# Attention of a four-layer kernel: tiles 8 to 15 are added to the four partial sums by accumulating DMAs, and the totals and the output product change slots

## What is computed

```python
scores = jnp.einsum('bhsd,bhtd->bhst', q, k) * scale
attn = jax.nn.softmax(scores, axis=-1)
o = jnp.einsum('bhst,bhtd->bhsd', attn, v_c)
o = o.transpose(0, 2, 1, 3).reshape(b, s, N_HEADS * D_K)
return o @ W_O + b_O
```

## Time and profile before

| | us |
|---|---|
| three runs | 737.27, 737.66, 738.73 |
| median | 737.66 |
| span of the profiled execution | 737.8 |
| attention loop in it, first score to last | 38.1 to 484.4 |

### The profile page before, as it was taken

How to read it: one execution, slowest core, us unless ns; L and a number is a source line. 1 busy time by engine, 2 the same in 40 slices (tenths; PEclk the granted TensorE clock), 3 DMA queues, 4 the chain that set the end, 5 groups by cost and what they waited for, 6 DMA issues and landing times.

```text
span 737.8 us, 12518 instructions
## 1 busy us (share of the span) xinstructions
PE 718.6 (97%) x4180; PEld 469.0 (64%) x4180; DVE 629.4 (85%) x1304; ACT 466.1 (63%) x1069; POOL 583.5 (79%) x484
## 2 busy tenths in 40 slices
PE   8999999999999999999999999999899999999997
PEld 7665655655656656556556555466666699778885
DVE  8889999999999999999999899765978736878885
ACT  4367766766767767767667676654777831455553
POOL 6489989999999999999989999963689861446774
PEclk9999999999999999999999999999999999999999
DMA  6300000000000000000000000012000000032431
GB/s 148 91 1 2 1 2 2 2 3 2 1 2 2 1 2 3 1 1 2 2 1 3 2 1 2 2 46 74 2 1 0 2 1 1 1 87 74 141 103 28
DMA packets 40679, 15.57 MB, mean 21 GB/s; under 512 B 27292, under 2 KB 36525, under 8 KB 40616
## 3 DMA queue, kind: packets, MB, share of 16 engines
q1 hardware_dynamic: 39336, 14.67, 8.2%
q10 hardware_dynamic: 1280, 0.12, 0.1%
HBM read 13.35 MB, written 1.10 MB: 20 GB/s over the span
## 4 chain that ended last, share of the span: by engine, by line
PE 74%; POOL 11%; issue 7%; DVE 6%; ACT 1%; DMA 0%; POOLq 0%; DVEq 0%
PE ps L1482 17%; PE ps L1468 16%; PE ps L1526 15%; POOL hid_lo L1007 5%; PE ps L1510 4%; PE ps L1880 4%; PE ps L1537 3%; POOL nrm L987 2%; DVE mx L1061 2%; PE ps L1920 2%; PE ps L1922 1%; PE ps L1921 1%; POOL hid L987 1%; PE ps L1455 1%; PE ps L1456 1%
## 5 line engine op out<-in xcount | busy, mean ns | idle before, releaser
L1061 DVE TENSOR_REDUCE mx<-ps 128x1 f32<-128x512 f32 x492 | 302.6, 681 | 14.7 <-PE ps L1468 13.2
L622 ACT ACTIVATE prob<-ps 128x512 f32<-128x512 f32 x512 | 262.7, 630 | 9.2 <-PE ps L1482 9.1
L1482 PE MATMUL ps<-q_cols,key 128*128 128x512 f32 x512 | 209.5, 412 | 0.8 <-ACT prob L622 0.8
L1468 PE MATMUL ps<-key,q_rows 128*128 128x512 f32 x512 | 204.7, 404 | 0.8 <-DVE key L1047 0.4
L901 POOL TENSOR_TENSOR part<-part,prob 128x512 f32<-128x512 f32 x124 | 158.6, 1290 | 30.4 <-DVE part L1076 25.9
L1482 PEld LDWEIGHTS ps<-q_cols,key 128*128 128x128 f32 x512 | 95.4, 187 | 89.5 <-issue 50.7
L1526 PE MATMUL ps<-prob,val 128*32 128x512 f32 x1024 | 124.1, 598 | 0.0
L1468 PEld LDWEIGHTS ps<-key,q_rows 128*128 128x128 f32 x512 | 95.6, 188 | 23.0 <-DVE mx L1061 5.5
L901 POOL TENSOR_TENSOR part<-part,pair 128x512 f32<-128x512 f32 x64 | 95.9, 1499 | 0.1
L1007 POOL TENSOR_TENSOR hid_lo<-hid,hid_hi 128x512 fp32r<-128x512 f32 x44 | 61.5, 1410 | 38.6 <-ACT hid_hi L785 38.6
L901 POOL TENSOR_TENSOR pair<-prob 128x512 f32<-128x512 f32 x64 | 82.7, 1293 | 1.9 <-ACT prob L622 1.8
(11 more groups left out here) (285 smaller groups left out, 1172.6 us busy)
## 6 DMA issues: line engine op xcount, KB each, us to landing
g_all<-g_rows SPq DMA_DIRECT2D x9, 256.0 KB, 3.3
den<-den_sb SPq DMA_DIRECT2D x124, 2.0 KB, 2.1
g_all<-g_rows SPq DMA_DIRECT2D x6, 224.0 KB, 3.0
X<-in_L_attn_h_t_dram SPq DMA_DIRECT2D x4, 256.0 KB, 4.5
out_dram<-X SPq DMA_DIRECT2D x4, 256.0 KB, 2.4
g_all<-g_rows SPq DMA_DIRECT2D x6, 128.0 KB, 3.1
g_all<-g_rows SPq DMA_DIRECT2D x4, 192.0 KB, 3.6
w_raw<-in_L_ffn_w_g_dram SPq DMA_DIRECT2D x1, 704.0 KB, 4.5
```

The lines of the kernel that those rows point to most:

```text
L622: act.activation(prob[:, g % RING, :], ps[:, g % 3, :], ACT.Exp, scale=SCALE).then_inc(s_exp, 1)
L1061: dve.tensor_reduce(mx[:, n % 2, c % TPB, at:at + 1], ps[:, BANK["rows", 2 * lin + j], :], AX.X, ALU.max).then_inc(s_mrd, 1)
L1468: pe.matmul(ps[:, BANK["rows", 2 * lin + j], :], q_rows[:, k, i * P:(i + 1) * P], key[:, h % KBUF, c0:c0 + BLK], start=True, stop=True).th ...
L1482: pe.matmul(ps[:, g % 3, :], key[:, n // NB % KBUF, t * P:(t + 1) * P], q_cols[:, n % NB, :], start=True, stop=True).then_inc(s_sc, 1)
```

## The change

GpSimd now makes two adds of 1024 columns in a block: tiles 0 and 1 with 4 and 5 into the partial sums 0 and 1, and tiles 2 and 3 with 6 and 7 into the sums 2 and 3 (`begin_sums`). Tiles 8 to 11 and then tiles 12 to 15 are added to all four sums by two accumulating DMAs of 128 rows by 2048 columns, issued from GpSimd's queue (`late_sums`). Each waits for the one before it (`s_late`). ScalarE waits on them before it overwrites tile 8 and tile 12. VectorE's two adds and `pair` are gone. `totals` adds the four partial sums in PSUM, with 16 products of 128 columns in place of four of 512, and 128 columns instead of 512 go on to `den_sb` and `den`, so VectorE's reduction is gone too. `totals` of block n - 2 stands in slot 1 and `output` of block n - 2 in slot 6. In the last block `totals` of block 29 stands in slot 1, its `output` behind slot 2, and `totals` of block 30 behind slot 4.

```diff
-        VSUM = (2, 3)
-        ADDS = NT - NG - len(VSUM)
+        LATE = 2
...
+        def begun(n):
+
+            return 2 * (n + 1)
...
-        def SUMS_AT(n):
-            return 6 if n < NBLK - 2 else 4
+        SUMS_AT, OUT_AT = 1, 6
...
-        for item, bank in ((("sums", NBLK - 1), 6), (("norm", 0), 3), (("sums", NBLK - 2), 5), (("out", NBLK - 2), 5), (("norm", 1), 4),
-                           (("out", NBLK - 1), 5)):
+        for item, bank in ((("sums", NBLK - 3), 4), (("out", NBLK - 3), 6), (("sums", NBLK - 2), 5), (("norm", 0), 3),
+                           (("out", NBLK - 2), 5), (("sums", NBLK - 1), 6), (("norm", 1), 4), (("out", NBLK - 1), 5)):
...
-                            sp.dma_start(den[:, n % 2, g, :], den_sb[C * g:C * g + 1, :].rearrange("a (p i) -> a p i", i=TPB)).then_inc(s_dend, 16)
+                            sp.dma_start(den[C * g:C * (g + 1), n % 2, :],
+                                         den_sb[C * g:C * g + 1, 0:P].rearrange("a (p i) -> a p i", i=TPB)).then_inc(s_dend, 16)
...
-                        act.copy(den_sb[:, :], ps[:, BANK["sums", n], :]).then_inc(s_densb, 1)
+                        act.copy(den_sb[:, 0:P], ps[:, BANK["sums", n], 0:P]).then_inc(s_densb, 1)
...
                     if g >= RING and t == 0:
                         act.wait_ge(s_pv, NW * (n - 1) + 1)
-                        act.wait_ge(s_sum, ADDS * (n - 1) + 5)
-                    elif g >= RING and t == NT // 2:
+                        act.wait_ge(s_sum, begun(n - 1))
+                    elif g >= RING and t == 2 * NG:
                         act.wait_ge(s_pv, NW * n)
-                        act.wait_ge(s_sum, ADDS * n)
+                        act.wait_ge(s_late, 16 * (LATE * (n - 1) + 1))
+                    elif g >= RING and t == 3 * NG:
+                        act.wait_ge(s_late, 16 * LATE * n)
...
+                def begin_sums(n, j):
+
+                    if n >= 2 and j == 0:
                         pool.wait_ge(s_ones, n - 1)
...
+                    ready(n, NG + 2 * j + 1)
+                    pool.tensor_tensor(part[:, n % 2, 2 * j:2 * j + 2, :], tiles(n, 2 * j, 2), tiles(n, NG + 2 * j, 2), ALU.add).then_inc(s_sum, 1)
+
+                def late_sums(n, j):
+
+                    ready(n, NG * (j + 3) - 1)
+                    if j == 0:
+                        pool.wait_ge(s_sum, begun(n))
+                    if LATE * n + j > 0:
+                        pool.wait_ge(s_late, 16 * (LATE * n + j))
+                    pool.dma_start(part[:, n % 2, :, :], tiles(n, NG * (j + 2), NG), accum_op=ALU.add).then_inc(s_late, 16)
...
                     bank_read(("sums", n))
-                    pe.wait_ge(s_sum, ADDS * (n + 1))
+                    pe.wait_ge(s_late, 16 * LATE * (n + 1))
                     for g in range(NG):
-                        last = pe.matmul(ps[C * g:C * (g + 1), BANK["sums", n], :], ones_v[:, :], part[:, n % 2, g, :], start=True, stop=True)
+                        for x in range(NG):
+                            last = pe.matmul(ps[C * x:C * (x + 1), BANK["sums", n], 0:P], ones_v[:, :], part[:, n % 2, g, x * P:(x + 1) * P],
+                                             start=(g == 0), stop=(g == NG - 1))
                     last.then_inc(s_ones, 1)
```

More of the change, by code:

```diff
@@ L241, in build_kernel @@
                     todo += [("folded", 0), ("folded", 1)]
-                if slot == 1 and 2 <= n < NBLK - 1:
+                if slot == SUMS_AT and 2 <= n < NBLK - 1:
+                    todo.append(("sums", n - 2))
+                if slot == OUT_AT and 2 <= n < NBLK - 1:
                     todo.append(("out", n - 2))
-                if slot == SUMS_AT(n) and 1 <= n < NBLK - 1:
-                    todo.append(("sums", n - 1))
-                if slot == 7 and n == NBLK - 2:
-                    todo.append(("out", n - 1))
             for item in todo:
@@ L652, in _ @@
                             sums(n - 1)
-                        if t == (2 * SUMS_AT(n) + 2 if n < NBLK - 1 else 8) and n >= 1:
+                        if t == 2 * SUMS_AT + 2 and n >= 2:
+                            sums_out(n - 2)
+                        if t == 10 and n == NBLK - 1:
                             sums_out(n - 1)
@@ L891, in _, with tiles @@
                 add_bias(3)
+                def tiles(n, first, count):
+                    at = (NT * n + first) % RING
+                    return prob[:, at:at + count, :]
                 def ready(n, tile):
                     pool.wait_ge(s_exp, NT * n + tile + 1)
-                def summed(n, count):
-                    pool.wait_ge(s_sum, ADDS * n + count)
-                def add(out, a, b):
-                    pool.tensor_tensor(out, a, b, ALU.add).then_inc(s_sum, 1)
-                def first_sums(n):
-                    def tile(t):
-                        return prob[:, (NT * n + t) % RING, :]
-                    total = [part[:, n % 2, g, :] for g in range(2)]
-                    if n >= 2:
-                        pool.wait_ge(s_ones, n - 1)
-                    ready(n, 1)
-                    add(total[0], tile(0), tile(1))
-                    ready(n, 3)
-                    add(pair[:, 0, :], tile(2), tile(3))
+                def begin_sums(n, j):
+                    if n >= 2 and j == 0:
+                        pool.wait_ge(s_ones, n - 1)
+                    ready(n, NG + 2 * j + 1)
+                    pool.tensor_tensor(part[:, n % 2, 2 * j:2 * j + 2, :], tiles(n, 2 * j, 2), tiles(n, NG + 2 * j, 2), ALU.add).then_inc(s_sum, 1)
@@ L915, in first_sums @@
+                def late_sums(n, j):
[5 more added lines that the diff above has]
+                    pool.dma_start(part[:, n % 2, :, :], tiles(n, NG * (j + 2), NG), accum_op=ALU.add).then_inc(s_late, 16)
+                for n in range(NBLK):
+                    begin_sums(n, 0)
                     if n < 2:
@@ L945, in _ @@
-                for n in range(NBLK - 1):
-                    first_sums(n)
-                    last_sums(n)
+                    begin_sums(n, 1)
+                    if n < NBLK - 1:
+                        late_sums(n, 0)
+                        late_sums(n, 1)
                     if n == NBLK - 2:
                         ln0_pool(pool, 0)
-                        ln0_pool(pool, 1)
-                first_sums(NBLK - 1)
-                summed(NBLK - 1, 5)
-                add(part[:, 1, 1, :], part[:, 1, 1, :], pair[:, 1, :])
@@ L1161, in _ @@
                                 queries_lo(n + 2, BANK["queries", n + 2])
-                        if slot == 1 and 2 <= n < NBLK - 1:
-                            denominators(n - 2)
-                            accumulate(n - 2)
                         if slot == 2 and n == 0:
@@ L1180, in _ @@
                             elif slot == 3:
+                                denominators(n - 2)
+                                accumulate(n - 2)
+                                ln0_stats(dve, 1)
+                            elif slot == 5:
                                 ln0_norm(dve, 1)
@@ L1554, in first_totals @@
                     n = NBLK - 1
-                    pe.wait_ge(s_sum, ADDS * n + 6)
-                    for g in range(2):
+                    pe.wait_ge(s_sum, begun(n))
+                    for g in range(NG):
                         pe.matmul(ps[C * g:C * (g + 1), BANK["sums", n], :], ones_v[:, :], part[:, n % 2, g, :], start=False, stop=False)
```

74 lines of the change are left out of this document (19 added, 55 removed).

## The result

The changed kernel takes 806.37 us (median of four runs, 805.88 to 810.31) against 737.47 before: a ratio of 1.094, with a 95% interval of 1.092 to 1.097. The forecast was 760, so it had the sign and the mechanism, but a third of the size.

The account below looks back on a forecast made before the run. TensorE's queue was taken to bound the loop, then the DMA chain: 737.8 us + 22.1 for the last block's wait on that chain + 0 for the other terms = 759.9, likeliest 760, range 738 to 865 (8 in 10).

Parts of the forecast that it names:

- D: Time of one accumulating 1 MiB DMA from issue to the wake-up of whoever waits: 7.25 us, bounds 4.5 to 9 and more.
- The formula of the text: End of the kernel as 737.8 + T - 479.0, where TensorE would reach the last `totals` at about 479 without waiting.
- T: When TensorE's wait for the 62nd DMA ends: later of 66.1 + 60 D and 470.2 + 2 D; 501.1 us forecast.
- the threshold: D = 6.97 us, where the chain of DMAs stops keeping up with the loop and begins to set its length.
- its own case: The DMA chain sets the loop, D from 6.97 to 8: 743 to 805 us, likeliest 760, chance 0.40.
- rival (c): The accumulating add is dearer than two reads, through the adding or GpSimd's descriptors: 805 us from D = 8, chance 0.20.
- the moves of slots change no work: On TensorE only `output` and `totals` change places, with 32-column products after slots 1 and 6 as before: cost 0.
- (a): The chain keeps up, D 5.3 to 6.97; only the last block waits for its `totals`: 741 us at D = 6, chance 0.27.
- (b): The second read is free or the chain short, D up to 5.3: 736 to 739.6 us, no difference, chance 0.13.
- The rival with the half rate: The accumulating DMAs add at half a copy's rate, 1 MiB in 4.2 us: D 6.0, 741 us, as in (a), chance 0.27.
- Landing of L918: Sign in the changed trace: the accumulating DMAs land after 7.25 us in the forecast case.
- GpSimd 43%: Sign: GpSimd's busy share falls from 79% to some 43% in the forecast case and in (a).

Follow-up runs that it names:

- e_none7: The changed kernel without its 62 DMAs (tiles 8 to 15 left out of the sum), `output` in slot 7 instead of 6: 736.15 us, ratio 0.996.
- e_one: The changed kernel with tiles 8 to 11 added by GpSimd and one accumulating 1 MiB DMA a block instead of two: 748.07 us, ratio 1.012.
- e_half2: The changed kernel with each accumulating DMA moving 512 KB instead of 1 MiB, the other half left out of the sum: 748.86 us (span 747.1).
- e_none: The changed kernel with its 62 DMAs taken out and nothing in their place, `output` still in slot 6: 743.51 us, ratio 1.007.

## Why the prediction was right and wrong

Up to the last score, the changed kernel needs 553.26 - 484.36 = 68.9 us more. Four differences of the table make it up: the change without DMAs and with `output` in slot 7, that is chiefly the adds taken away, 482.50 - 484.36 = -1.9; `output` in slot 6, 489.53 - 482.50 = +7.0; the chain in the loop, 529.40 - 476.61 = +52.8; the last block, 23.86 against 12.92 us = +10.9. Sum 68.9. Behind the last score 1.6 us come back by the clock (251.81 against 253.45), and the span grows by 67.3.

**Right: what decides.** TensorE bounded the loop, the saved adds were worth nearly nothing (1.9 us here, 2.7 by the ratio of `e_none7`), and one chain of two links a block set the new time. The failed step is the size of D: 7.25 us in the sum, 7.99 measured. The formula of the text, 737.8 + T - 479.0, gives 804.7 with the measured T of 545.9, against 805.1. But that it comes out so close is luck in part: from T to `output` of block 30 the text had 5.6 us and the trace has 553.49 - 545.95 = 7.5, since TensorE runs at half its clock behind the wait, and the 1.6 us of clock at the end hide most of that.

**Wrong: D.** It was 1.72 fixed + 2 x 2.72 + 0.1 = 7.25 us; a link is 7.99. The landing was put at 7.15 and is 7.40, the start of the next link at 0.1 and is 0.55 to 0.58. The second was taken from ScalarE's wake-up, but the waiter is GpSimd with a DMA to issue, and no row showed that lead. The shortest landing is 6.8 us, under the estimate; the mean is 7.40. With one DMA a block it is much the same, 7.42 in `e_one`, although its median is 7.0 there: most land near 7.0 and some up to 9.1. What makes those late is open. SyncE's small `den` DMAs are no clear cause: 30 of the 31 landings of `e_one` have all four of them issued meanwhile. Sixty links turned 0.73 us into 44 of the 45 us that were missing (805.1 - 759.9). The text noted that its D was 4% over the threshold; by its own formula each tenth of a microsecond above it is 6 us, and that made a likeliest time of 760 so weak. The result lies on the border that the text drew between its own case and rival (c), an add dearer than two reads (805 us from D = 8). Of (c) the runs bear out that GpSimd adds to the link (0.55 us), and not that the add itself costs more than twice the copy's data.

**Wrong, and hidden by it: "the moves of slots change no work".** The group of products was the same, but the bank that `output` takes was not: 7.0 us up to the last score. It doesn't show in the changed kernel, where the chain covers it; it shows as soon as the chain is short. For rivals (a) and (b) the text gave 741 and 736 to 739.6 us. `e_half2` has a link of 5.0 us (4.4 + 0.55), in rival (b)'s range, and takes 747.1: against the 737.8 before these are -1.9 for the adds, 7.0 for the slots, 5.8 in the last block and -1.6 of clock at the end. In the last block the text saw the wait for the totals (1.99 us) and not the one for the layer norm beside it (1.79).

**The rival with the half rate** (a reduce step at half a copy's rate, by the Trainium skill, Collectives: The Full Stack, Part 3, an estimated D of 6.0) had the ratio right: the data part doubles, 2.4 to 4.8 us. It was the fixed 2.0 and GpSimd's lead that made the link 8 and not 6.

**The signs.** DMA share 7 tenths or more: 5 to 7, mean 0.66. Landing of L918 7.25: 7.40. ScalarE waits for landings: 137.6 us. First scores 14.5 us apart: 16.0. TensorE 94%: 92%. GpSimd 43%: 47%, since the 62 DMA instructions count as busy with 54.6 us and an add takes 2.63 us on the mean and not 2.37 (2.38 in `e_none`, 2.72 for the 26 that start within 1 us of a DMA). The totals cost 0.02 us a block, not 0.07. The small DMA into `q_cols` lands in 3.6 us instead of 1.9 (median) in the changed kernel, where 30 of the 32 go out while a large one is under way; TensorE's first scores wait for it 3.5 us in all. In the kernels whose chain keeps up it lands in 1.9 as before.

## What to carry to other kernels

A chain of DMAs that wait for each other is costed by its link: landing and the issuer's lead, times the links, against the time that the bound engine needs for the same work. Where the two are close, as 14.5 against 13.88 us were here in the forecast, a small error in the link is paid once per link, so cut it into independent chains before anything else: the same bytes in two chains gave back 53 of 69 us. And an operation moved to another slot has to be followed to its buffer's last reader; it costs nothing where its engine has work, but it can wait for a bank that nobody has emptied.

## What the runs showed of the hardware

A DMA of 1 MiB from SBUF to SBUF, issued by GpSimd, lands after 4.4 us as a copy and after 6.8 as an add; 512 KB added after 4.4. GpSimd shows 0.55 us before each such DMA and 0.88 us in it (0.56 for a copy), and it takes the next add before the transfer has landed. Two VectorE operations of 0.34 us took 2.39 and 2.52 us beside GpSimd adds of 2.35 and 2.33. Behind a wait of 7.36 us TensorE's granted clock was 0.50 for 2 us, and 32 products took 1.94 us instead of 1.05. Single landings were 1.8 to 2.2 us late where one DMA was in flight (6.2 against 4.4, 9.0 against 6.8) and up to 3.7 with two (8.2 against 4.4); what delays the single ones is open.
